# TensorE's sum of a unit: two units behind its queries at the end of a step, in place of three at its head

## What is computed

```
xn = layernorm(h)                                  # nodes
Q, K, V = xn @ wq + bq, xn @ wk + bk, xn @ wv + bv # 8 heads of 32
w_phys = (silu(rbf @ w1 + b1) @ w2 + b2) * cutoff  # edges
msg_phys = xn[col] * w_phys
scores = sum(Q[row] * K[col], -1) / sqrt(32) * cutoff
attn = softmax(scores, over the 8 heads)
combined = msg_phys + gate * attn * V[col]
aggr = segment_sum(combined, row)
out = x + h + aggr @ wo + bo
```

## Time and profile before

| | us |
|---|---|
| median of 3 runs | 5507.02 |
| lowest and highest | 5505.51, 5512.03 |
| the profiled execution | 5505.26 |
| its span | 5503.4 |
| PE busy | 5147.0 (94%) |
| DVE busy | 4196.1 (76%) |
| ACT busy | 3928.7 (71%) |
| POOL busy | 3871.3 (70%) |

### The profile page before, as it was taken

How to read it: one execution, slowest core, us unless ns; L and a number is a source line. 1 busy time by engine, 2 the same in 40 slices (tenths; PEclk the granted TensorE clock), 3 DMA queues, 4 the chain that set the end, 5 groups by cost and what they waited for, 6 DMA issues and landing times. The chain is left out here.

```text
span 5503.4 us, 117739 instructions
## 1 busy us (share of the span) xinstructions
PE 5147.0 (94%) x24352; PEld 3858.7 (70%) x24353; DVE 4196.1 (76%) x7422; ACT 3928.7 (71%) x12602; POOL 3871.3 (70%) x3476
## 2 busy tenths in 40 slices
PE   3779999999999999996799999999999999999999
PEld 3556666666666666674577777777777777777777
DVE  9889987666655555323688888888888888888895
ACT  4555666666666666665688888888888888888883
POOL 1567777777777777776577777777777777777770
PEclk9999999999999999998899999999999999999999
DMA  6233444444444443444899999999999999999966
GB/s 200 94 108 130 149 165 159 143 151 166 158 143 150 166 159 135 153 153 168 289 326 330 330 332 335 331 329 332 330 332 330 336 331 334 330 330 334 333 203 187
DMA packets 584395, 1306.11 MB, mean 237 GB/s; under 512 B 81246, under 2 KB 384134, under 8 KB 582961
## 3 DMA queue, kind: packets, MB, share of 16 engines
q0 software_dynamic: 221536, 881.08, 44.3%
q1 hardware_dynamic: 311796, 345.48, 21.0%
q10 hardware_dynamic: 50850, 77.03, 3.9%
HBM read 1024.15 MB, written 324.38 MB: 245 GB/s over the span
## 5 line engine op out<-in xcount | busy, mean ns | idle before, releaser
L1030 POOL DMA_INDIRECT ukvx<-kvx_table,urec x1760 | 2058.7, 1170 | 737.6 <-issue 663.6
L339 POOL DMA_INDIRECT records<-rows,slot_i x1660 | 1745.5, 1051 | 672.4 <-issue 470.0
L694 PE MATMUL w_ps<-w2s,hid 128*128 128x256 f32 x6656 | 1544.8, 386 | 51.6 <-DVE rows L608 51.6
L694 PEld LDWEIGHTS w_ps<-w2s,hid 128*128 128x128 f32 x6656 | 1243.0, 192 | 372.9 <-issue 156.2
L608 DVE TENSOR_TENSOR rows<-w_ps,b2b 128x512 f32<-128x512 f32 x832 | 571.0, 686 | 737.9 <-PE w_ps L694 737.8
L808 ACT ACTIVATE hid<-hid_ps,b1t 128x512 f32<-128x512 f32 x832 | 526.2, 683 | 811.3 <-PE hid_ps L683 796.9
L1133 PE MATMUL uq_ps<-aggr,uonehotT 128*128 x3520 | 976.9, 400 | 88.4 <-issue 72.7
L1153 PE MATMUL ag_ps<-ukvx,uonehot 128*128 128x256 f32 x3520 | 982.8, 402 | 0.2 <-issue 0.2
L1156 PE MATMUL ag_ps<-ukvx,uonehot 128*128 128x256 f32 x3520 | 907.1, 380 | 0.7 <-DVE ukvx L1249 0.6
L1074 ACT ACTIVATE uexp<-uscores,umax 128x8 f32<-128x8 f32 x1760 | 507.3, 289 | 402.2 <-DVE umax L1233 399.7
L829 ACT ACTIVATE rows<-rows 128x256 f32<-128x256 f32 x1664 | 706.7, 504 | 66.7 <-DVE rows L608 66.7
(11 more groups left out here) (176 smaller groups left out, 5069.9 us busy)
## 6 DMA issues: line engine op xcount, KB each, us to landing
urec<-records SPq DMA_DIRECT2D x880, 260.0 KB
rbf_in<-in_edge_attr SPq DMA_DIRECT2D x207, 256.0 KB, 3.0
kvx_table<-kvx ACTq DMA_DIRECT2D x10, 3456.0 KB
ukvx<-kvx_table,urec POOLq DMA_INDIRECT x1760
records<-rows,slot_i POOLq DMA_INDIRECT x1661, 2.5
records<-kvx SPq DMA_DIRECT2D x1, 13000.0 KB
aggr<-query_table SPq DMA_DIRECT2D x7, 1792.0 KB, 19.2
fbase<-x_plus_h SPq DMA_DIRECT2D x14, 896.0 KB, 7.1
```

Source lines behind the costliest of these rows:

```text
L339: pool.indirect_dma_start(recs, bass.IndirectOffsetOnAxis(ap=slot_i[:, q, t:t + 1], axis=0), rows[:, q, t, :], None).then_inc(scattered[q] ...
L694: m = pe.matmul(w_ps[j % 2][:, h, :], hid[:, k % 2, c, h, j * P:(j + 1) * P], w2s[:, c, :], start=(h == 0 and c == 0), stop=(c == 1), skip ...
L1030: pool.indirect_dma_start(kvx[:, k, j, :], None, table, bass.IndirectOffsetOnAxis(ap=rec[:, k, j, R_DST:R_DST + 1].bitcast(I32), axis=0), ...
```

## The change

`LAG`, by which TensorE's sum trails the unit of the step, becomes 2. The old value stays for ScalarE under the name `KLAG`, and the padding of the table (`HPAD`) goes by it, so ScalarE's code does what it did. In TensorE's step the sum and its register load move from the head to the end, directly ahead of the renewal. The register load for the queries moves ahead of the transposes. In the very first step the first two queries move ahead of the transposes of unit 3. After the loops two sums are left over instead of three.

```diff
-LAG = 3
+LAG = 2
+KLAG = 3
 QLAG = 2
-HPAD = 2 * LAG + 4
+HPAD = 2 * KLAG + 4
...
             def unit(u, k, i, first, last):
                 half = k % 2 * 2
-                if k % 2 == 0:
-                    summed[:] = four(half_bucket, u * 2 + (HPAD - 2 * LAG), mybir.EngineType.PE)
-                if not (first and k < LAG):
-                    aggregate(u - LAG, (k - LAG) % DEPTH, summed[half:half + 2])
-                ahead(turn, TURN_AHEAD, u, k, i, first, last)
+                late = last and k + ASK_AHEAD >= DEPTH
                 if first and k == 0:
                     asking[:] = four(half_asked, 0, mybir.EngineType.PE)
                     for n in range(ASK_AHEAD):
                         query(n, n, asking[2 * n:2 * n + 2], True)
                 if first and 2 * (k + ASK_AHEAD) == QC:
                     pe.wait_ge(q_first[1], 16)
-                if not (last and k + ASK_AHEAD >= DEPTH):
-                    if k % 2 == 0:
-                        asking[:] = four(half_asked, u * 2 + 2 * ASK_AHEAD, mybir.EngineType.PE)
+                if k % 2 == 0 and not late:
+                    asking[:] = four(half_asked, u * 2 + 2 * ASK_AHEAD, mybir.EngineType.PE)
+                ahead(turn, TURN_AHEAD, u, k, i, first, last)
+                if not late:
                     query(u + ASK_AHEAD, (k + ASK_AHEAD) % DEPTH, asking[half:half + 2], first and k + ASK_AHEAD < DEPTH)
+                if k % 2 == 0:
+                    summed[:] = four(half_bucket, u * 2 + (HPAD - 2 * LAG), mybir.EngineType.PE)
                 if not (first and k < LAG):
+                    aggregate(u - LAG, (k - LAG) % DEPTH, summed[half:half + 2])
                     renew_next(u - LAG, summed[half + 1])
```

More of the change, by code:

```diff
@@ L1099, in unit @@
                 if k % 2 == 0:
-                    bucket_of[:] = four(half_bucket, u * 2 + (HPAD - 2 * LAG), mybir.EngineType.Activation)
+                    bucket_of[:] = four(half_bucket, u * 2 + (HPAD - 2 * KLAG), mybir.EngineType.Activation)
                 ahead(evacuate, OUT_AHEAD, u, k, i, first, last)
@@ L1106, in unit @@
                 ahead(pick, SPREAD_AHEAD - 1, u, k, i, first, last)
-                if not (first and k < LAG):
-                    keep(u - LAG, bucket_of[k % 2 * 2])
+                if not (first and k < KLAG):
+                    keep(u - KLAG, bucket_of[k % 2 * 2])
             turns(act, unit)
-            for n in range(LAG):
+            for n in range(KLAG):
                 if n % 2 == 0:
-                    bucket_of[:] = four(half_bucket, HALVES + 2 * n + (HPAD - 2 * LAG), mybir.EngineType.Activation)
-                keep(UNITS - LAG + n, bucket_of[n % 2 * 2])
+                    bucket_of[:] = four(half_bucket, HALVES + 2 * n + (HPAD - 2 * KLAG), mybir.EngineType.Activation)
+                keep(UNITS - KLAG + n, bucket_of[n % 2 * 2])
             act.wait_ge(s["ag_done"], UNITS)
```

## The result

The changed kernel takes 5630.69 us (median, from 5627.72 to 5631.76) against 5509.52 us for the kernel before in the same runs (5505.51 to 5512.51). The ratio is 1.022, with an interval from 1.0207 to 1.0233: slower by 121 us, where 5506 and no change were predicted. Lines of `edges` have moved down by one: L1212 answers to L1211, L1217 to L1216, L1134 to L1133, L1154 and L1157 to L1153 and L1156, L1138 to L1137, L961 to L960.

What follows compares the result with a forecast made beforehand. The prediction took VectorE to bound the kernel. To the profiled 5505.26 us it added terms of 0, 1 and 0, giving about 5506 us and no change, with a range of 5490 to 5522.

Steps and rivals of the forecast that it cites:

- VectorE bounds the kernel; idle time of PE is a trap: In the steady stage VectorE sets the pace, 3.106 us a unit; PE's 65.5 us idle before queries costs it nothing.
- the list of signs: Signs to seek in the changed kernel's trace, among them VectorE's busy and idle time per unit unchanged to 0.02 us.
- The order written out: PE's new sequence: renewal ahead of the transposes, sum between the same two groups as before; matmul work 0 us.
- The split of 0.78 us: Time from transposes to even query, split into L, the register load, and a, one group's address arithmetic and issue.
- rival B: The sum behind the even query gets later, buffers free later, more gathers land late: 5520 to 5535 us, chance 0.17.
- The term a + L + a: Time from even query to its sum: 0.88 to 1.13 us against 0.97 before; costed at +1 us.
- The wait itself is thus covered.: The renewal's wait for ScalarE's copy ends at 4005.22, before the transposes' copy at 4005.49; costed at 0.
- The price of a late sum: Late gather landings: 55 waits over 440 pairs, each changed by the sum's shift, -12 to +30 us, middle +1.
- A: Rival: gathers start earlier, so 5493 us, or 5479 if all landing waits went; chance 0.14.
- C: Rival: sums run a unit earlier, or PE sets the pace and its gaps close: 5415 us, chance 0.03.
- The start of the stage and the last units: Query waits at the stage's start change by under 2 us in all, last two steps unchanged; costed at 0.
- If VectorE waits for queries in the steady part: Sign in the changed kernel's trace that the renewal's wait holds back more than worked out; before, such waits were 0.3 us.

Runs made afterwards that it cites:

- e1: The changed kernel with the sum's register load read from a 16-byte-aligned place in the queries' table: 5525.26 us, ratio 1.0026.
- e17: The changed kernel with ScalarE's copy moved ahead of the exponentials in its step, slow load kept: 5504.06 us, ratio 0.9987.
- e18: The changed kernel with the sum's load aligned and ScalarE's copy moved ahead of the exponentials: 5485.44 us, ratio 0.9956.
- e5: The kernel before with only the register load for the queries moved ahead of the transposes: 5493.30 us, ratio 0.9968.
- e3: The kernel before with 32 register loads added behind the last sum, four at each of eight table entries, each with a tiny matmul: 5538.50 us.
- e2: The kernel before with the sum's numbers loaded from a table copy shifted by two entries, off the boundary, order unchanged: 5510.41 us, ratio 1.000.
- e7: The changed kernel with lighter gathers, 2 KB a row in place of 3, node features left out: 5509.29 us, ratio 0.9998.
- e13: The changed kernel with the slow load done for the next pair behind the even sum, in three pairs of four: 5653.75 us, ratio 1.0254.

## Why the prediction was wrong, point by point

- **VectorE bounds the kernel; idle time of PE is a trap.** Right, and it held to the end: VectorE's waits alone give the loss (124 us by the rows), and with the same 237 us of gaps on TensorE the kernel took 5631 or 5504 us. Idle time per unit to 0.02 us, as the list of signs had it, was wrong by 0.15.
- **The order written out.** Right: renewal ahead of the transposes, the gap ahead of the even query gone (65.5 to 0.0), lost time ahead of the even sum.
- **The split of 0.78 us.** I bounded the load by 0.43 and 0.68 and never measured it, though the sequencer's rows of the kernel before had it: 333 ns. The rest, 0.45 us, is arithmetic and waits. How good this part was shows in e1, where the load kept its 333 ns: its even sum begins 1.05 us behind the query on average (0.88 to 1.13 were worked out), and in three pairs of four 2.36 us behind the copy (1.88 to 2.38, from 4005.22 to 4007.10 and 4007.60). It lost 14 us, near the 15 of rival B's first figure.
- **The term a + L + a, with L carried over to its new place.** The first step that failed. The load's address moved with `LAG`, off a boundary of four entries, and L became 1.007. The sum begins 1.25 us behind its query at 4006.70, and 1.53 on average over 296 even sums, where 0.88 to 1.13 was worked out. The Trainium skill ("DMA: Bandwidth & Descriptors", section "Latency and other measured facts") gives such a load a floor of about 600 ns; the rows show 332 ns, below that floor, and 1007, and the measurement decides.
- **"The wait itself is thus covered."** The second step that failed, and the dearer one. I compared the copy's end (4005.22) with the end of the copy that the transposes wait for (4005.49), and found a later gate behind an earlier one. I did see the chain behind it and followed it to the sum, but as a shift of one pair against a fixed copy, and priced the wait at 0. Two things were missing. The wait takes away the lead with which loads and arithmetic ran ahead under the queued matmuls, and it does so in every pair, at a copy that itself follows VectorE's maximum. And at the loop's head the branch stands in the chain, 207 ns by its own row and arithmetic around it: there the even sum begins 3.49 us behind the copy, against 2.94 in the other pairs (2.82 against 2.36 with the load aligned). With the copy moved out of the way, and nothing changed on TensorE, the time fell by 127 us with the slow load (e17) and by 40 us with the fast one (e18 against e1). That is what the runs show for a term that I had at 0.
- **The price of a late sum.** The mechanism of rival B was right: sum late, buffer late, gather late, VectorE waits. Its size was not: 55 landings times the shift, doubled at most, gave 30 us. The count went from 40 to 107 and the length from 0.48 to 0.86 us. B also had its point of decision in the wrong quantity: a (0.21) in place of L.
- **Rivals A, B and C.** B had the direction and a chance of 0.17, but its 5520 to 5535 us are far from 5631. VectorE's wait for gathers grew, so A didn't come about, and TensorE's order was as written out, so C didn't. e5 shows that A's gain was there to be had, by the place of the asking load alone: 17 us, between A's 12 and 26.
- **The start of the stage and the last units.** Costed at 0, and nothing in the result asks for more: the steady window's rate accounts for the loss.
- **The list of signs.** "If VectorE waits for queries in the steady part, the renewal's wait holds back more than I worked out" pointed at the right place, in part by luck. The 12.4 us in 23 waits stood in the first view of the changed kernel, and they go with the renewal's wait (e17 has none). But 10.0 us of them come by way of the clock, which the prediction doesn't mention. I took them for a side effect and came to the renewal only in the last two runs.

## What to carry to other kernels

When a lag or an offset changes, look at the address of every register load that depends on it: here four entries off a 16-byte boundary took three times as long, and the sequencer's rows tell it. When a wait is moved, ask not only whether it is met in time but what stands behind it in the same stream: here loads and address arithmetic that ran ahead under queued matmuls began only when it opened, and the engine still looked busy. Count the branch at the loop's head with them. And an engine's gaps are no measure of a loss: ask how far ahead of the bounding engine the buffers are given back, read as the waits of the engine that starts the transfers.

## What was unexpected in the hardware

- A load of four table entries into TensorE's registers takes 332 ns from a multiple of 16 bytes and 995 to 1005 ns from the six other places tried (e3).
- 1.0 us of such a load in each of 440 pairs costs nothing where the stream has a lead (e2: 5510.41 against 5511.96; e17: 5504.06), and with the wait in front of it the changed kernel takes 5630.69.
- With the DMA engines at 0.93 of their time 107 late landings cost 0.86 us each (3 KB a row), at 0.80 of their time 91 cost 0.29 each (2 KB, e7). The sums were less late in e7 as well.
- In the middle of a stage in which TensorE is over 90% busy its granted clock fell to 0.50 (1.2 GHz) for a stretch, behind 3.70 us in which it had been busy for 2.11, and VectorE then waited for queries. The changed kernel has twelve such stretches in 2000 us, e13 thirty-four, the kernel before and e17 none.
